# The last three shared tiles of a decoder layer: accumulating transfers in place of read back, addition and store

## The chip, the core and the metric

One core of one Trainium2 chip runs the whole kernel. The metric is the device time of one execution in microseconds. The core's engines work beside each other, each on its own list of instructions: TensorE (PE in the profile; its weight loads are PEld), VectorE (DVE), ScalarE (ACT), GpSimd (POOL) and SyncE (SP), which here does nothing but start transfers. They wait for each other on semaphores. Transfers between the memory outside the core (DRAM here) and the core's own memory (SBUF) are started by SP (the profile's queue q1, "hardware") or by POOL (queue q0, "software": POOL itself first writes the descriptors of the transfer, and the profile shows that time as a busy POOL). Both feed the same 16 DMA engines.

## The reference, cut to what matters

```
x = x + attention(layernorm(x))                 # 16 heads, causal, soft cap, gates
x = x + token_experts(layernorm(x))             # 4 experts, chosen by token id
x = x + moe(layernorm(x))                       # the last stage

def moe(h):                                     # h: 2048 rows of 512
    probs = softmax(h @ gate_w.T)               # 8 experts, the best 2 of each row
    out = silu(h @ shared_gate.T) * (h @ shared_up.T) @ shared_down.T
    y = silu(h @ expert_gate) * (h @ expert_up) @ expert_down
    return out + sum of the 2 chosen y, weighted
```

The output is 2048 x 512 floats. Each of its rows is a sum of four things: the residual x that enters the last stage, the shared expert's row, and two rows of routed experts.

## The kernel before, in words

The 2048 rows are 16 tiles of 128. In the last stage TensorE first computes the up-products of the shared expert for all 16 tiles, then their down-products for 13 of them. `resid` holds x, tile by tile; `shared_add` (DVE) adds the shared row to it out of a PSUM bank, and SP stores the tile to `out`. Then come the routed experts: the chosen rows are sorted by expert into ETILES = 39 tiles of 128. For each of them POOL gathers the rows (`gather`), TensorE computes, ScalarE copies the product to `x3_early`, and POOL adds it to the rows of `out` where it belongs, in DRAM, with an indirect transfer that accumulates (`add_rows`, L866). Each of these adds waits until the one before has landed (`e_added`), since two tiles may hold the same row of the output.

The down-products of three shared tiles are left for the very end (LATE = 3; they are steps n = 13, 14 and 15 of `down_s`, and by `PLACES` they are the tiles 12, 13 and 14 of the output). They fill TensorE while the last routed tiles go through the other engines. Since the routed rows for these three tiles are added in DRAM as well, x for them is stored to `out` early, with one transfer (L687). At the end SP waits for the last of the 39 adds, reads the three tiles back from `out` to `resid` (L701), DVE adds the shared product from its bank (L1555, banks 3, 0 and 1), and SP stores the three tiles again (L704). SP then waits until the three stores have landed, and the program ends.

What sets the order around the change is the order in which each engine's instructions are written, and the semaphores: `e_added` (39 adds, 16 each), `s_y` (a shared down-product is complete in its bank), `s_y_out` (DVE has taken it), `stored` (SP's early stores), `late_loaded` and `late_stored`. No scheduler moves anything.

Of the kernel before, what the change touches and what calls it, by code (L numbers as in the profile page):

```python
# [7 lines left out]
ALU = mybir.AluOpType  # L8
# [6 lines left out]
TILES = T // P  # L15
# [26 lines left out]
EARLY_FROM, LATE_FROM = 6, 12  # L42
LATE = 3
# [4 lines left out]
ETILES = TOPK * T // P + EXPERTS - 1  # L48
# [20 lines left out]
def build(nc, x, token_ids, wqk_in, wv_in, wgates, wo_in, pre, out):  # L69
    with ExitStack() as ctx:  # L70
# [21 lines left out]
        def sem(name):  # L92
            return ctx.enter_context(nc.semaphore(name))

        bank = [ctx.enter_context(nc.psum_tensor(f"bank{i}", [P, 512], F32)) for i in range(8)]
# [3 lines left out]
        resid = sb("resid", [P, TILES, D])  # L99
# [183 lines left out]
        S = {n: sem(n) for n in names.split()}  # L283
# [111 lines left out]
        ov = out[0:T].rearrange("(t p) d -> p t d", p=P)  # L395
# [35 lines left out]
        PLACES = [*range(LATE_FROM), TILES - 1, *range(LATE_FROM, TILES - 1)]  # L431
        LATE_AT = TILES - LATE
        LATE_BANKS = (3, 0, 1)

        def odd(n):

            return FULL_STEPS <= n < LATE_AT and (n - FULL_STEPS) % 2
# [16 lines left out]
        def y_bank(n):  # L454
            if n >= LATE_AT:
                return LATE_BANKS[n - LATE_AT]
            return XT if n >= FULL_STEPS and not odd(n) else YB
# [15 lines left out]
        def _(sp):  # L473
# [181 lines left out]
            def load_expert(e):  # L655
                at = EXP_AT + e * (UP + DOWN)
                if e == 2:
                    sp.wait_ge(S["route_e_done"], 1)
                if e >= 2:
                    tiles_before = sp.value_load(expert_end[0:1, e - 2:e - 1], min_val=1, max_val=ETILES)  # L660
                for part, used, lo, n in (("up", "e_up", 0, UP), ("down", "e_aT_ready", UP, DOWN)):
                    if e:
                        sp.wait_ge(S[f"{part}_loaded"], 16 * e)
                    if e >= 2:
                        sp.wait_ge(S[used], tiles_before + (used == "e_aT_ready"))
                    sp.dma_start(plain(expert_w[:, e % 2, 2 * lo:2 * lo + 2 * n].rearrange("p (l n) -> p l n", l=2)),
                                 pre_parts[:, :, at + lo:at + lo + n]).then_inc(S[f"{part}_loaded"], 16)
# [28 lines left out]
                sp.dma_start(ov[:, PLACES[n], :], resid[:, PLACES[n], :]).then_inc(S["stored"], 16)  # L696
            for e in range(2, EXPERTS):
                load_expert(e)
            sp.wait_ge(S["e_added"], 16 * ETILES)
            for n in range(LATE):  # L700
                sp.dma_start(resid[:, LATE_FROM + n, :], ov[:, LATE_FROM + n, :]).then_inc(S["late_loaded"], 16)  # L701
            for n in range(LATE_AT, TILES):
                sp.wait_ge(S["s_y_out"], n + 1)
                sp.dma_start(ov[:, PLACES[n], :], resid[:, PLACES[n], :]).then_inc(S["late_stored"], 16)  # L704
            sp.wait_ge(S["late_stored"], 16 * LATE)

        @block.gpsimd
        def _(pool):
# [139 lines left out]
            def gather(g):  # L848

                if g < 2:  # L850
                    pool.wait_ge(S["s_xT_ready"], TILES - 1 + g)
                else:
                    pool.wait_ge(S[f"e_row{g % 2}"], 16 * (g // 2))
                before = g - ROW_BUFFERS
                if before >= 0:
                    pool.wait_ge(S["e_xT_ready"], before + 1)
                    if not by_tensor(before):
                        pool.wait_ge(S["e_moved"], before - TB + 1)
                nc.gpsimd.indirect_dma_start(rows_e(g), None, x3_rows, bass.IndirectOffsetOnAxis(ids_e[:, g:g + 1], 0)).then_inc(S[f"e_row{g % 2}"], 16)

            def add_rows(g):

                pool.wait_ge(S["e_y_out"], g + 1)
                if g:
                    pool.wait_ge(S["e_added"], 16 * g)
                nc.gpsimd.indirect_dma_start(out, bass.IndirectOffsetOnAxis(ids_e[:, g:g + 1], 0), x3_early[:, g % E_ROWS, :], None, compute_op=ALU.add).then_inc(S["e_added"], 16)  # L866
# [8 lines left out]
            for g in range(ETILES):  # L875
                if g + ROW_BUFFERS < ETILES:
                    gather(g + ROW_BUFFERS)
                add_rows(g)

        @block.scalar  # L880
        def _(act):
# [289 lines left out]
        def _(dve):  # L1171
# [376 lines left out]
                turn(x3(t)).then_inc(S["s_xT_ready"], 1)  # L1548

            def shared_add(n):  # L1550
                if n >= LATE_AT:
                    dve.wait_ge(S["late_loaded"], 16 * LATE)
                dve.wait_ge(S["s_y"], n + 1)
                row = resid[:, PLACES[n], :]
                nc.vector.tensor_tensor(row, bank[y_bank(n)][:, :], row, ALU.add).then_inc(S["s_y_out"], 1)  # L1555

            def turn_rows_e(t):
# [8 lines left out]
            def step(ph, g, j=0, first=False, last=False, between=None):  # L1566
                W, H = WIDTH[ph], HALVES[ph]
                for i in range(H):
                    dve.wait_ge(S[f"{ph}_silu"], H * g + i + 1)
                    part = act_sb[:, i * W:i * W + W]  # L1570
                    if ph == "e":
                        nc.vector.scalar_tensor_tensor(out=part, in0=bank[1][:, 0:W], scalar=weights_e[:, g:g + 1], in1=part, op0=ALU.mult, op1=ALU.mult).then_inc(S["e_act"], 1)
                    else:
                        nc.vector.tensor_tensor(part, part, bank[X_FIRST if first else 0][:, 0:W], ALU.mult).then_inc(S["x_act"], 1)
                if not last:
                    xT_low(ph, g + 1)
                if ph == "e" and first:
                    shared_add(LATE_AT - 1)
                if between:
                    between()  # L1580
                if ph == "e":
                    weights_ready("down_loaded", g)
                last_x = last and ph == "x"
                parts = LAST_PARTS_X if last_x else aT_parts(ph)
                for n, (c0, c1) in enumerate(parts):
                    w = chunk(ph, c0)[1]
                    of = last_bank(c0, c1) if last_x else aT_bank(ph, c0, c1, w)

                    read = n + 1 if last_x else sum(p[0] // KC <= c0 // KC for p in parts)
                    dve.wait_ge(S[f"{ph}_aT_hi"], len(aT_parts(ph)) * g + read)  # L1590
                    nc.vector.tensor_tensor(aT_lo[0:w, c0:c1, :], of, aT_hi[0:w, c0:c1, :].bitcast(F32), ALU.subtract).then_inc(S[f"{ph}_aT_lo"], 1)
# [80 lines left out]
            def step_s(g):  # L1672
                mult_s(g, 0)
                if g + 1 < TILES:
                    xT_low_s(g + 1)
                mult_s(g, 1)
                if 1 <= g <= FULL_STEPS:
                    shared_add(g - 1)
                if g < FULL_STEPS:
                    aT_low_s(g)  # L1680
                if TURNED_FROM <= g + 2 < TILES:
                    turn_x3(g + 2)
# [105 lines left out]
            choose(FIRST_ROUTED, TILES)  # L1788
            nc.vector.tensor_tensor(by_router.chosen[:, :], choice[0][:, :], choice[1][:, :], ALU.add).then_inc(S["chosen_ready"], 1)
            shared_add(FULL_STEPS)  # L1790
            aT_low_s(FULL_STEPS + 2)
            link(nc.vector.tensor_copy(share_hi[:, :, :], share[:, :, :]))
# [43 lines left out]
        def _(pe):  # L1836
# [220 lines left out]
            def down(ph, g, hi, lo, second, between=None, to=YB, parts=None):  # L2057
                if second:
                    pe.wait_ge(S[f"{ph}_y_out"], g)
                parts = parts or aT_parts(ph)  # L2060
                for c in range(NCH[ph]):
                    w = chunk(ph, c)[1]
                    if c == NCH[ph] - 1 and between:
                        between()
                    for n, (c0, _) in enumerate(parts):
                        if c == c0:
                            pe.wait_ge(S[f"{ph}_aT_lo"], len(aT_parts(ph)) * g + n + 1)
                    last = triple(bank[to][:, :], aT_hi[0:w, c, :], aT_lo[0:w, c, :], hi(c, w), lo(c, w), c == 0, c == NCH[ph] - 1)
                last.then_inc(S[f"{ph}_y"], 1)
# [235 lines left out]
```

## Time and profile before

| | us |
|---|---|
| time before, median of 3 runs | 1555.71 (1552.31 to 1561.29) |
| the profiled execution, its own time | 1548.69 |
| its span | 1546.9 |
| PE busy | 1523.6 (98%) |
| DVE busy | 1163.8 (75%) |
| ACT busy | 655.6 (42%) |
| POOL busy | 454.0 (29%) |
| last matmul started | 1534.94 |
| first instruction of the final exchange (SP, L701) | 1537.84 |

The span is the time from the first to the last instruction in the trace; the execution's own time is 1.8 us longer. Time stamps in this document count from the start of the span. A busy share is an average over the whole span, and says nothing of the last few microseconds, where the change is; those are read from the timeline and the chain of waits.

### The profile page before, as it was taken

Reading aid. Unit: us, or ns where it says so; the run is one execution under the profiler, and the core shown is the slowest. Engines: PE = TensorE matmul, PEld = TensorE weight load, DVE = VectorE, ACT = ScalarE, POOL = GpSimd, SP = SyncE. Lnnn points to the kernel's source line nnn. Section 1 sums busy time; section 2 is a strip of 40 time slices with the busy share of each in tenths; the row PEclk is TensorE's granted clock in tenths of the full one; section 3 lists DMA queues with packets and bytes.
Section 4 is the critical chain, followed back from the end, with each engine's and each line's share of the span. In section 5 each row is a group of like instructions: output and inputs, shape, how many; then the busy total and the mean of one; then the engine's idle time right before and its main releaser. Section 6 shows DMA issues by size and latency. Waiting matters only on the chain.

```text
span 1546.9 us, 24256 instructions
## 1 busy us (share of the span) xinstructions
PE 1523.6 (98%) x7597; PEld 1309.7 (85%) x7598; DVE 1163.8 (75%) x2609; ACT 655.6 (42%) x1277; POOL 454.0 (29%) x391
## 2 busy tenths in 40 slices
PE   8999999999999999999999999999999999999996
PEld 7778888888888888888888888888888889999995
DVE  4898887788887888887888778755663675777772
ACT  4454443444444334444344444333111315666662
POOL 4445332234222233222233231113210003333332
PEclk9999999999999999999999999999999999999998
DMA  8786763687986686885686878376441157778744
GB/s 315 283 307 222 236 230 130 239 310 261 303 302 220 252 315 248 310 315 203 257 308 258 318 278 321 99 227 194 131 153 43 50 211 225 231 232 262 196 80 79
DMA packets 106843, 353.98 MB, mean 229 GB/s; under 512 B 11312, under 2 KB 31792, under 8 KB 101232
## 3 DMA queue, kind: packets, MB, share of 16 engines
q1 hardware_dynamic: 93520, 314.62, 56.0%
q0 software_dynamic: 13216, 38.02, 10.4%
q8 instruction: 57, 0.93, 0.3%
q14 instruction: 50, 0.41, 0.1%
HBM read 228.34 MB, written 124.26 MB: 228 GB/s over the span
## 4 chain that ended last, share of the span: by engine, by line
PE 87%; DMA 5%; DVE 5%; issue 1%; POOL 1%; ACT 1%; SPq 0%; DVEq 0%; POOLq 0%; ACTq 0%
PE bank L399 28%; PE bank L400 28%; PE bank L401 28%; DMA out<-x_early,ids_e 4%; PE bank L2079 1%; DMA wqk<-wqk_parts 1%; PE bank L1910 0%; DMA rows<-x_rows,ids_e 0%; DMA wv_raw<-wv_in 0%; POOL store L721 0%; DVE resid L1555 0%; DVE place_hot L1727 0%; DVE tile_vals L1737 0%; DVE stats L1181 0%; DMA resid<-out 0%
## 5 line engine op out<-in xcount | busy, mean ns | idle before, releaser
L765 POOL TENSOR_TENSOR probs<-probs,causal 128x256 f32<-128x256 f32 x126 | 90.3, 738 | 401.9 <-ACT probs L951 390.6
L399 PE MATMUL bank<-store,wqk 128*128 128x512 f32 x512 | 200.3, 391 | 0.8 <-DMA wqk<-wqk_parts 0.8
L400 PE MATMUL bank<-store,wqk 128*128 128x512 f32 x512 | 200.0, 391 | 0.0
L401 PE MATMUL bank<-store,wqk 128*128 128x512 f32 x512 | 199.2, 389 | 0.0
L1351 DVE SCALAR_TENSOR_TENSOR resid<-bank,factor,resid 128x512 f32<-128x512 f32 x256 | 189.1, 741 | 1.8 <-PE bank L401 1.7
L721 POOL TENSOR_TENSOR pre_split<-pre_raw,pre_split 128x1536 fp32r<-128x1536 f32 x34 | 119.4, 3512 | 137.6 <-ACT pre_split L910 137.6
L949 ACT ACTIVATE probs<-bank 128x512 f32<-128x512 f32 x189 | 86.8, 527 | 128.6 <-PE bank L401 125.7
L401 PEld LDWEIGHTS bank<-store,wqk 128*128 128x128 f32 x512 | 96.2, 188 | 20.5
L399 PEld LDWEIGHTS bank<-store,wqk 128*128 128x128 f32 x512 | 96.3, 188 | 19.7 <-DMA wqk<-wqk_parts 1.2
L1000 ACT ACTIVATE k_hi<-bank 128x512 fp32r<-128x512 f32 x64 | 38.4, 600 | 175.3 <-PE bank L401 175.3
L400 PEld LDWEIGHTS bank<-store,wqk 128*128 128x128 f32 x512 | 96.4, 188 | 17.7
L1379 DVE TRANSPOSE_TENSOR_REDUCE bank<-probs 128x16 f32<-128x512 f32 (+3 forms) x256 | 108.5, 492 | 0.0
L399 PE MATMUL bank<-wo,o_hi 128*128 128x512 f32 x256 | 103.9, 406 | 2.5 <-issue 0.9
L399 PE MATMUL bank<-expert_w,xT_hi 128*128 x312 | 103.8, 333 | 1.1 <-DVE xT_lo L1538 0.8
L866 POOL DMA_INDIRECT out<-x_early,ids_e x39 | 61.6, 1579 | 146.1 <-DMA out<-x_early,ids_e 78.6
L399 PE MATMUL bank<-store 128*128 128x512 f32 x256 | 100.2, 392 | 1.1 <-DVE store L1335 1.1
L400 PE MATMUL bank<-expert_w,xT_hi 128*128 x312 | 100.4, 322 | 0.0
L401 PE MATMUL bank<-expert_w,xT_lo 128*128 x312 | 100.3, 322 | 0.0
L400 PE MATMUL bank<-wo,o_hi 128*128 128x512 f32 x256 | 100.0, 391 | 0.0
L401 PE MATMUL bank<-wo,o_lo 128*128 128x512 f32 x256 | 99.9, 390 | 0.0
L401 PE MATMUL bank<-store 128*128 128x512 f32 x256 | 99.7, 389 | 0.0
L400 PE MATMUL bank<-store 128*128 128x512 f32 x256 | 99.7, 389 | 0.0
(366 smaller groups left out, 3983.3 us busy)
## 6 DMA issues: line engine op xcount, KB each, us to landing
pre_parts<-pre_split SPq DMA_DIRECT2D x34, 1536.0 KB, 6.5
wqk<-wqk_parts SPq DMA_DIRECT2D x96, 512.0 KB, 4.3
pre_raw<-pre SPq DMA_DIRECT2D x34, 768.0 KB, 8.2
store<-wv_parts SPq DMA_DIRECT2D x12, 2048.0 KB, 9.2
wo<-wo_parts SPq DMA_DIRECT2D x48, 512.0 KB, 7.1
expert_w<-pre_parts SPq DMA_DIRECT2D x8, 2816.0 KB, 11.1
wqk_parts<-wqk SPq DMA_DIRECT2D x16, 1024.0 KB, 5.6
expert_w<-pre_parts SPq DMA_DIRECT2D x8, 1536.0 KB
```

What stands on the lines that cost most here:

```text
L399: nc.tensor.matmul(out_ap, a_hi, b_hi, start=first, stop=False)
L400: nc.tensor.matmul(out_ap, a_hi, b_lo, start=False, stop=False)
L401: return nc.tensor.matmul(out_ap, a_lo, b_hi, start=False, stop=last)
L721: nc.gpsimd.tensor_tensor(lo, raw, hi.bitcast(F32), ALU.subtract).then_inc(S[done], 1)
L765: nc.gpsimd.tensor_tensor(diagonal, diagonal, causal[:, :, :], ALU.mult).then_inc(S["masked"], 1)
L866: nc.gpsimd.indirect_dma_start(out, bass.IndirectOffsetOnAxis(ids_e[:, g:g + 1], 0), x3_early[:, g % E_ROWS, :], None, compute_op=ALU.add) ...
L949: nc.scalar.activation(probs[:, lo:lo + n], bank[2 + i][:, 0:n], ACT.Tanh, scale=SCALE / SOFTCAP).then_inc(S["tanh_done"], 1)
L1000: nc.scalar.activation(k_hi[:, :], bank[1][:, :], ACT.Copy).then_inc(S["qk_hi_done"], 1)
L1351: nc.vector.scalar_tensor_tensor(out=row, in0=bank[of][:, :], scalar=factor[:, u % 2, i:i + 1], in1=row, op0=ALU.mult, op1=ALU.add).then_i ...
L1379: last = nc.vector.tensor_reduce(sums[:, j * P // BLOCK:, 0, j], cols, mybir.AxisListType.X, ALU.add, apply_transpose=True)
L2079: last = nc.tensor.transpose(bank[AT + c // KC][0:w, c % KC * P:c % KC * P + P], act_of_chunk(ph, c), ident[:, :])
```

## The change

The read back, the addition on DVE and the plain store of the three late tiles go. Instead DVE copies the shared product from its bank to the tile of `resid` as soon as it is complete (and once the early store of that tile has landed), and POOL, after the last of the 39 adds has landed, starts three direct transfers that accumulate these tiles onto `out` in DRAM. SP only waits for the three transfers.

```diff
@@ -696,12 +696,6 @@
             for e in range(2, EXPERTS):
                 load_expert(e)
-            sp.wait_ge(S["e_added"], 16 * ETILES)
-            for n in range(LATE):
-                sp.dma_start(resid[:, LATE_FROM + n, :], ov[:, LATE_FROM + n, :]).then_inc(S["late_loaded"], 16)
-            for n in range(LATE_AT, TILES):
-                sp.wait_ge(S["s_y_out"], n + 1)
-                sp.dma_start(ov[:, PLACES[n], :], resid[:, PLACES[n], :]).then_inc(S["late_stored"], 16)
             sp.wait_ge(S["late_stored"], 16 * LATE)
@@ -876,6 +870,10 @@
                 add_rows(g)
+            pool.wait_ge(S["e_added"], 16 * ETILES)
+            for n in range(LATE_AT, TILES):
+                pool.wait_ge(S["s_y_out"], n + 1)
+                nc.gpsimd.dma_start(ov[:, PLACES[n], :], resid[:, PLACES[n], :], accum_op=ALU.add).then_inc(S["late_stored"], 16)
@@ -1548,10 +1546,12 @@
             def shared_add(n):
-                if n >= LATE_AT:
-                    dve.wait_ge(S["late_loaded"], 16 * LATE)
                 dve.wait_ge(S["s_y"], n + 1)
                 row = resid[:, PLACES[n], :]
+                if n >= LATE_AT:
+                    dve.wait_ge(S["stored"], 16 * (LATE_AT + 1))
+                    nc.vector.tensor_copy(row, bank[y_bank(n)][:, :]).then_inc(S["s_y_out"], 1)
+                    return
                 nc.vector.tensor_tensor(row, bank[y_bank(n)][:, :], row, ALU.add).then_inc(S["s_y_out"], 1)
```

On SP, at the end of its list, the change takes out the transfers of the final exchange (the difference between before and after):

```order
 L665 REGISTER_ALU [waits down_loaded]
 L666 DMA expert_w<-pre_parts 128x2x1536 [waits e_aT_ready]
-L701 DMA resid<-out 128x512 [waits e_added]
-L701 DMA resid<-out 128x512 x2
-L704 DMA out<-resid 128x512 [waits s_y_out] x3
 L70 UNCONDITIONAL_BRANCH [waits late_stored]
```

Six transfers have gone, three loads and three stores; the last row, which is SP's wait for the end, stays.

On POOL, at the end of its list, before the change (L866 is `add_rows`, L859 `gather`):

```order
L866 DMA out<-x_early,ids_e 2176x512 [waits e_added,e_y_out]
L859 DMA rows<-x_rows,ids_e 128x512 [waits e_moved,e_xT_ready,e_row1]
L866 DMA out<-x_early,ids_e 2176x512 [waits e_added,e_y_out]
L859 DMA rows<-x_rows,ids_e 128x512 [waits e_moved,e_xT_ready,e_row0]
L866 DMA out<-x_early,ids_e 2176x512 [waits e_added,e_y_out] x8
L70 UNCONDITIONAL_BRANCH
```

The same place on POOL after the change, where L860 is `add_rows` and L853 `gather`:

```order
L860 DMA out<-x_early,ids_e 2176x512 [waits e_added,e_y_out]
L853 DMA rows<-x_rows,ids_e 128x512 [waits e_moved,e_xT_ready,e_row0]
L860 DMA out<-x_early,ids_e 2176x512 [waits e_added,e_y_out] x8
L876 DMA out<-resid 128x512 [waits s_y_out,e_added]
L876 DMA out<-resid 128x512 [waits s_y_out] x2
L70 UNCONDITIONAL_BRANCH
```

The three accumulating transfers stand behind everything else that POOL does. On DVE the three additions at the end of its list have become three copies in the same place, and TensorE's and ScalarE's lists are unchanged.

## Rows read from the trace of the kernel before

**Rows 1.** The page: the span, and the busy time of each engine

```profile
span 1546.9 us, 24256 instructions
PE 1523.6 (98%) x7597; PEld 1309.7 (85%) x7598; DVE 1163.8 (75%) x2609; ACT 655.6 (42%) x1277; POOL 454.0 (29%) x391
```

**Rows 2.** Chain that ended last, 1490 to 1548 us: start, length, what

```profile
by line: DMA out<-x_early,ids_e 73.8%; issue 12.1%; DMA resid<-out 6.3%; DVEq L70 1.8%; SPq L701 1.3%; DVE resid L1555 1.1%; POOLq L70 0.4%; POOLq L865 0.2%; DVEq L1553 0.0%
...
1527.80 4.57 DMA out<-x_early,ids_e
...
1533.18 4.64 DMA out<-x_early,ids_e
...
1538.72 3.67 DMA resid<-out
```

**Rows 3.** Timeline of SP, same stretch: start, length, queue, line, what

```profile
1537.84 1.31 SPq L701 DMA_DIRECT2D resid<-out  x3
1543.13 1.53 SPq L704 DMA_DIRECT2D out<-resid  x3
```

**Rows 4.** Line L704, the last stores: durations ns, first and last start; landing

```profile
L704 SPq DMA_DIRECT2D out<-resid x3: 332/338/343, 1543.1 to 1544.3; - x3
...
DMA to landing us min/median/max: 2.0/2.1/2.2
```

**Rows 5.** Timeline of DVE, 1527 to 1548 us

```profile
1529.63 0.89 DVE L1669 TENSOR_TENSOR aT_lo_odd<-bank,aT_hi_odd 128x512 fp32r<-128x512 f32 x2 [4.70 <-ACT aT_hi_odd L1142]
1530.55 0.29 DVE L1670 TENSOR_TENSOR aT_hi_odd<-bank,aT_hi_odd 64x128 fp32r<-64x128 f32 x1
1542.41 1.89 DVE L1555 TENSOR_TENSOR resid<-bank,resid 128x512 f32<-128x512 f32 x3 [11.56 <-DMA resid<-out]
```

**Rows 6.** Timeline of TensorE from 1531 us: tile 14's last matmul, tile 15's last

```profile
1531.09 0.39 PE L2175 MATMUL bank<-sh_down_lo,aT_hi_late 128*128 128x512 f32 x1
...
1534.94 0.39 PE L2175 MATMUL bank<-sh_down_lo,aT_hi_odd 128*128 128x512 f32 x1
```

**Rows 7.** Timeline of POOL, 1505 to 1548 us, the last two adds

```profile
1527.80 1.55 POOL L866 DMA_INDIRECT out<-x_early,ids_e  x1 [4.12 <-DMA out<-x_early,ids_e]
1533.18 1.55 POOL L866 DMA_INDIRECT out<-x_early,ids_e  x1 [3.83 <-DMA out<-x_early,ids_e]
```

**Rows 8.** Line L866, the 39 accumulating adds: POOL ns min/median/max; landing

```profile
L866 POOL DMA_INDIRECT out<-x_early,ids_e x39: 1549/1580/1647, 1287.5 to 1533.2; - x39
...
DMA to landing us min/median/max: 4.5/4.8/10.9
```

**Rows 9.** Line L770, indirect plain stores on POOL, same columns

```profile
L770 POOL DMA_INDIRECT xs<-xrows,slot_x x16: 960/972/1201, 339.5 to 998.1; - x16
```

**Rows 10.** Line L819, direct plain loads of 384 KB on POOL, same columns

```profile
L819 POOL DMA_DIRECT2D sh_down_lo<-pre_parts x4: 546/546/548, 1059.5 to 1066.0; - x4
...
DMA to landing us min/median/max: 3.4/3.9/5.8
```

**Rows 11.** Timeline of POOL, 1040 to 1130 us, a pair of these loads

```profile
1059.48 1.08 POOL L819 DMA_DIRECT2D sh_down_lo<-pre_parts  x2 [4.87 <-DVE bank L1197]
```

**Rows 12.** Timeline of DVE, 1058 to 1060 us, what that pair waited for

```profile
1058.10 1.09 DVE L1197 STREAM_TRANSPOSE bank<-rows 128x512 f32<-128x512 f32 x1
```

**Rows 13.** Engines by stretch; the last two columns: DMA share, GB/s

```profile
1535.30:1537.40 2.10, 0.03 (x1) 0.00 (x0) 0.00 (x0) 0.00 (x0) 0.00 (x0) 1.00 1.02 125
1537.84:1538.84 1.00, 0.00 (x0) 0.00 (x0) 0.00 (x0) 0.00 (x0) 0.00 (x0) 0.58 0.02 6
1538.84:1542.34 3.50, 0.00 (x0) 0.00 (x0) 0.00 (x0) 0.00 (x0) 0.00 (x0) 0.50 0.72 223
1543.80:1546.30 2.50, 0.00 (x0) 0.00 (x0) 0.50 (x1) 0.00 (x0) 0.00 (x0) 0.50 0.85 315
```

**Rows 14.** The last add's transfer in slices of half a microsecond, same columns

```profile
1535.80:1536.30 0.50, 0.00 (x0) 0.00 (x0) 0.00 (x0) 0.00 (x0) 0.00 (x0) 1.00 0.27 49
1536.30:1536.80 0.50, 0.00 (x0) 0.00 (x0) 0.00 (x0) 0.00 (x0) 0.00 (x0) 1.00 1.05 193
1536.80:1537.30 0.50, 0.00 (x0) 0.00 (x0) 0.00 (x0) 0.00 (x0) 0.00 (x0) 1.00 1.01 184
```

## The prediction

> **What bounds the kernel now.** I read the page's span and busy times first, then the chain that ended last, then the timelines of SP, DVE, TensorE and POOL over the last 20 us, and last the lines whose operations resemble the new one. TensorE is busy 98% of 1546.9 us [rows 1], so nearly all of the kernel is its matmuls, and the change leaves its list alone. Its last matmul starts at 1534.94 and lasts 0.39 [rows 6]: some 11.6 us of span lie behind it, in which TensorE does nothing, and the edit is in there.
>
> In the last 57 us the chain runs through the accumulating adds, 73.8% of it [rows 2], one behind another: an add is issued at 1527.80, the next at 1533.18, the engine idle 3.83 us between for the landing [rows 7]. The last lands at 1533.18 + 4.64 = 1537.82 [rows 2]; call it T, since SP starts its first read back at 1537.84 [rows 3]. The sum is made from there, and everything ahead of T is the same in both kernels: the same 39 adds behind the same waits.
>
> The exchange at the end: SP issues three loads from 1537.84 for 1.31 us [rows 3]; the last lands at 1538.72 + 3.67 = 1542.39 [rows 2]; DVE, idle 11.56 us for it, adds three tiles from 1542.41 for 1.89 us [rows 5]; the three stores are issued from 1543.13, the last at 1544.3, and land 2.0 to 2.2 us later [rows 3, 4], so at about 1546.4; the span ends at 1546.9 [rows 1]. So the tail is 1546.9 - 1537.84 = 9.06 us: 4.6 load, 1.9 DVE and the issue of the last store, 2.1 landing, 0.5 from there to the end.
>
> **What goes.** All of the 9.06 us but the last 0.5: 8.6 us. SP's removed wait has nothing behind it but the wait for the end. No load is left to start after T.
>
> **What moves under cover.** The three DVE copies. A copy of 128x512 from a bank is close to the addition of that size, 1.89/3 = 0.63 us [rows 5]. They stand where the additions stood, behind DVE's last split, which ends at 1530.55 + 0.29 = 1530.84 [rows 5]. The first two can run as soon as tile 14's last matmul is over, 1531.09 + 0.39 = 1531.5 [rows 6], the third after 1534.94 + 0.39 = 1535.33, so all are done by about 1536.0 to 1536.1. That is 1.7 us before T, and I put them at nothing; if that cover went, the price would be what the third exceeds T by. The added wait on `stored` asks for the count that the 39 adds wait for as well (L874), and the first of them was issued at 1287.5 [rows 8]: it costs nothing. Three semaphore waits on POOL stand behind all its other work; nobody is queued behind them but the three transfers.
>
> **What is added on the path.** Three direct accumulating transfers of 256 KB. No row of this trace is one; there are indirect accumulating ones (L866), indirect plain ones (L770) and direct plain ones (L819), all on POOL. Four terms:
>
> - From T to POOL's first instruction. Before an add it is 1533.18 minus the landing at 1527.80 + 4.57 = 1532.37: 0.8 us [rows 2]. [...] Bounds 0.3 and 0.8; I take 0.8, the same semaphore on the same engine.
> - Writing descriptors. Direct plain: 0.55 us each, two in 1.08 with no gap [rows 10, 11]. Indirect plain 0.97, indirect accumulating 1.58, the last one 1.55 [rows 7 to 9]: accumulation adds 0.6. So 0.55 + 0.6 = 1.15 us; bounds 0.55 and 1.55.
> - From the end of that to landing. The last add: 4.64 - 1.55 = 3.1 us [rows 2, 7]; the shortest direct load, larger but plain: 3.4 - 0.55 = 2.85 [rows 10]. I take 3.1.
> - What the second and third add. Their descriptors are written while the first is moving, so the spacing is the larger of 1.15 us and what the DMA engines need for one. The last add keeps them active for 2.1 us [rows 13], but not evenly: after a first burst there is a lull of half a microsecond at a share of 0.27, and then they move 184 to 193 GB/s [rows 14]. The lull looks like the first answer to the read of the destination, which a transfer queued behind another need not wait for by itself. At 188 GB/s 262,144 bytes take 1.4 us. Plain stores take 0.85 x 2.5 / 3 = 0.7 us each [rows 13]. Bounds: 0.7 below (a plain transfer's share; with the low descriptor time), 2.1 above if they pipeline; 4.65 if they don't (a rival below). I take 1.4, twice 2.8.
>
> Sum from T: 0.8 + 1.15 + 3.1 + 2.8 = 7.85, with the 0.5 at the end 8.35 us. Against 9.06: -0.7 us. The saving of two dependent round trips (load, then store) is given back by slower descriptors and slower, read-and-write transfers. With all low bounds: 0.3 + 0.55 + 2.85 + 1.4 + 0.5 = 5.6, so -3.5. With the high ones, pipelined: 0.8 + 1.55 + 3.1 + 4.2 + 0.5 = 10.15, so +1.1.
>
> A rule that gives another figure: the Trainium skill, "DMA: Bandwidth & Descriptors", section "Anatomy of one DMA", fits a software-queue transfer as about 2.0 us plus its bytes at 436 GB/s, which would be 2.6 us for 256 KB. This trace disagrees for accumulating ones: none of 39 landed in under 4.5 us [rows 8]. By the rule's figure, with two more at 0.6 us of movement each, an estimate of the tail is 0.8 + 2.6 + 1.2 + 0.5 = 5.1 us, near that of the first rival below.
>
> **Forecast.** The profiled execution's own time is 1548.69; less 0.7 it is 1548.0. It lies 7.0 us under the median of the three runs, so at the level of that median the forecast is 1555.0. The difference is 0.05%: no change that can be told. A measurement of this kernel can tell about 0.5%, 7.8 us, from no change; the three runs before lie 9.0 us apart.
>
> **Rivals.**
>
> 1. *Three accumulates cost hardly more than three plain transfers.* Then the low bounds hold: -3.5 us, 1552.2. For it: the direct form's 0.55 us of descriptors, and the 315 GB/s of the stores' stretch [rows 13]. Against it: each add carries the destination's read too, and ran at 0.6 of that speed [rows 14]. Still under 0.5%.
> 2. *The accumulates serialise.* The engines don't start reading the destination of one before the write of the one before it is confirmed, so each takes its whole 4.65 us: 0.8 + 1.15 + 3.1 + 2 x 4.65 + 0.5 = 14.85, +5.8 us, 1561.5: slower than before. Place: the DMA queue behind POOL's second and third transfer. It decides from a spacing of (9.06 - 0.5 - 5.05) / 2 = 1.75 us up: above that the change loses. For it: no two adds are ever in flight together here, so the trace can't exclude it. Against it: plain software transfers overlap (two loads are issued within 1.08 us and land after 3.9 in the median [rows 10, 11]).
>
>    The Trainium skill, same page, section "Two DMAs through the same engine are not ordered", says that descriptors of one queue start in order but are pipelined, read and write sides apart. By that rule the spacing would stay at 1.4 and not 4.65; no row here shows it for accumulating ones.
> 3. *A direct accumulate is cut into smaller pieces than the indirect one.* Say four times the descriptors, 4.6 us for each: 0.8 + 3 x 4.6 + 3.1 + 0.5 = 18.2, +9.1 us, 1564.8. For it only that no such transfer is in the trace, and that some adds landed after 10.9 us [rows 8]; against it, both sides are whole rows of 2 KB.
> 4. *The change doesn't do what it says*: POOL is late because the third copy is, and T is not what it waits for. The copy has 1.7 us of cover; if TensorE's end moved by that much, both kernels would move alike. Price under 1 us.
>
> **How the numbers follow.** Forecast (tail 7.6 to 10.2 us) 50%, own range 1550 to 1560 with the runs' spread; rival 1, 23%; rival 2, 19%; rival 3, 5%; rival 4, 3%. All mechanisms but the third stay within 7.8 us, so what leads out of "same" is chiefly the spread of runs: of the forecast, about a twelfth to either side; of rival 1 a sixth to the faster side; of rival 2 a quarter to the slower side; of rival 3 two thirds. That gives faster 0.09, slower 0.13, same 0.78. Range: from 1552.2 less some 3 us of spread, to rival 2's 1561.5: 1549 to 1561.5.
>
> **What would show it.** In the profile after: the last add landing with the same distance to TensorE's end; three DVE copies of about 0.63 us done before it; three POOL instructions of 1.1 to 1.2 us, back to back, 0.8 us (or 0.3) behind it; the DMA engines active in one unbroken stretch of some 4 to 5 us (rival 1: 2 to 3; rival 2: three stretches with gaps); the third landing 7.9 us after T; no SP transfer behind the expert weights. The forecast is wrong if the tail is outside 7.6 to 10.2 us, or if the loop of adds itself takes another time.

## The result, and the profile after

| | before | after |
|---|---|---|
| median of 22 runs each, us | 1553.45 (1547.87 to 1561.29) | 1557.80 (1552.24 to 1561.77) |
| ratio, 95% interval | | 1.0027 [1.0016, 1.0038] |
| profiled execution: own time, span, us | 1548.69, 1546.9 | 1557.56, 1555.8 |
| T, landing of the last of the 39 adds | 1537.83 | 1543.18 |
| tail, from T to the end of the span | 9.1 | 12.6 |

The change makes the kernel slower by 0.27%, 4.2 us (2.5 to 5.9), where 0.7 us less was forecast. That is less than the 0.5% that the forecast took for the smallest difference to be told; with 22 runs of each it is clear of noise, and the sign was wrong. The two profiles lie 8.9 us apart, and 3.5 of it is tail. The other 5.4 us is T, and nothing here puts it down to the edit. small_soft, tile_waits, its repeat tile_waits_b, two_queues and small_soft3 below have the kernel before's lists up to T, and their T is 1542.4, 1542.4, 1544.8, 1540.9 and 1548.3, against 1537.8 in the profile of before; load_behind has the changed kernel's lists up to T, and its T is 1537.1. Most of the shift is there before the last adds: TensorE's last matmul starts at 1534.94 before [rows 6] and at 1539.31 after, 4.4 us later.

```profile
1539.31 0.39 PE L2175 MATMUL bank<-sh_down_lo,aT_hi_odd 128*128 128x512 f32 x1
```

What moves TensorE's end and T from one execution to the next was not studied. So everything below is measured from T.

The end of the chain of waits in the changed kernel (start, length, what):

```profile
1538.61 4.57 DMA out<-x_early,ids_e
1543.18 1.17 issue
1544.34 1.88 POOL out L876 x2
1546.22 0.89 POOLq L70
```

It answers to the chain of [rows 2], where the load stood behind the last add. The chain is followed to POOL's third transfer and its closing instruction, 1546.22 + 0.89 = 1547.11, and then stops, 8.7 us ahead of the end: a hint that what comes next isn't an ordinary instruction. POOL's timeline and DVE's, which answer to [rows 7] and [rows 5]:

```profile
1538.61 1.56 POOL L860 DMA_INDIRECT out<-x_early,ids_e  x1 [3.98 <-DMA out<-x_early,ids_e]
1544.34 2.77 POOL L876 DMA_DIRECT2D out<-resid  x3 [4.18 <-issue]
```

```profile
1535.24 1.33 DVE L1553 COPY resid<-bank 128x512 f32<-128x512 f32 x2
1539.73 0.69 DVE L1553 COPY resid<-bank 128x512 f32<-128x512 f32 x1 [3.16 <-PE bank L2175]
```

The copies are done at 1540.42, 2.8 us ahead of T: they cost nothing, as forecast. Line L876 (POOL's time for one in ns, then the time from start to landing), which answers to [rows 8]:

```profile
L876 POOL DMA_DIRECT2D out<-resid x3: 961/1267/1597, 1544.3 to 1545.5; - x3
...
DMA to landing us min/median/max: 3.9/5.3/6.1
```

The three rows of POOL overlap (they start at 1544.34, 1544.96 and 1545.52), so that the three together take 2.77 us and not the sum of their durations. The third is started at 1545.5 and lands 6.1 later, at 1551.6. After that there is nothing to move, and still 4.2 us to the end. The engines and the DMA share by stretch, as in [rows 13] (the DMA engines are active for 5.9 us without a gap, where the forecast said 4 to 5):

```profile
1545.30:1551.20 5.90, 0.00 (x0) 0.00 (x0) 0.00 (x0) 0.00 (x0) 1.81 (x3) 0.50 0.92 133
1551.60:1555.60 4.00, 0.00 (x0) 0.00 (x0) 0.00 (x0) 0.00 (x0) 0.00 (x0) 0.50 0.00 0
```

SP's waits at the end (engine, line, what it waited for: us in total, times, longest) show who is late:

```profile
SPq L70 <- DMA out<-resid: 105.6, 1, 105.6
SPq L70 <- PEq L70: 4.0, 1, 4.0
```

Once the transfers have landed, SP waits another 4.0 us in the barrier that closes the program (L70), where each engine reports after its own drain. In the kernel before, the same row says 0.2. The engine that the row names is a guess by its semaphore; TensorE's last matmul had ended at 1539.7. The rows of line L70 itself (queue, operation, ns, start) say which it was. After, and then before:

```profile
L70 POOLq EVENT_SEMAPHORE  x2: 17/17/17, 1555.6 to 1555.7; - x2
L70 ACTq DRAIN  x1: 901/901/901, 1533.4 to 1533.4; - x1
L70 PEldq DRAIN  x1: 4267/4267/4267, 1535.5 to 1535.5; - x1
L70 DVEq DRAIN  x1: 730/730/730, 1539.7 to 1539.7; - x1
L70 POOLq DRAIN  x1: 10402/10402/10402, 1545.2 to 1545.2; - x1
L70 SPq COMPARE_BRANCH  x1: 37/37/37, 1551.6 to 1551.6; - x1
```

```profile
L70 POOLq EVENT_SEMAPHORE  x2: 17/17/17, 1546.7 to 1546.8; - x2
...
L70 POOLq DRAIN  x1: 8914/8914/8914, 1533.0 to 1533.0; - x1
...
L70 SPq COMPARE_BRANCH  x1: 38/38/38, 1546.5 to 1546.5; - x1
```

POOL's drain stands behind its last transfer in POOL's list in both, though its row begins up to 0.3 us before that transfer's own row. Before, it runs from 1533.0 to 1541.9, four microseconds beyond T, but SP's exchange lasts to 1546.5 and hides it. After, it runs to 1555.6, 4.0 beyond the last landing. The drains of ScalarE, TensorE and DVE had ended by 1540.5, and SP is through its own wait at 1551.6: POOL's is the only one left, and the program ends 0.2 behind it. In all eight profiles of this document in which POOL's drain is the last to end, the span ends 0.23 us behind it. This long row was in the trace of before; it was hidden there, and I didn't ask what hid it.

### The profile page after: what moved, and what is told of

Same layout as the page of the kernel before. It is cut to its first block, busy times and chain, and to the rows that moved or that the text cites. A ratio compares the mean times of both kernels' runs of the same rounds, so it can differ in the third digit from the quotient of the medians.

```text
span 1555.8 us, 24254 instructions
## 1 busy us (share of the span) xinstructions
PE 1525.6 (98%) x7597; PEld 1309.8 (84%) x7598; DVE 1164.5 (75%) x2609; ACT 655.9 (42%) x1277; POOL 457.7 (29%) x394
## 4 chain that ended last, share of the span: by engine, by line
PE 84%; DMA 7%; DVE 5%; issue 2%; POOL 1%; ACT 1%; POOLq 0%; SPq 0%; DVEq 0%; ACTq 0%
PE bank L399 27%; PE bank L400 27%; PE bank L401 27%; DMA out<-x_early,ids_e 5%; DMA wqk<-wqk_parts 1%; PE bank L2079 1%; PE bank L1910 0%; DMA rows<-x_rows,ids_e 0%; DMA wv_raw<-wv_in 0%; POOL store L715 0%; DVE place_hot L1727 0%; DVE tile_vals L1737 0%; DMA x_early<-xs_out,slot_x 0%; DVE resid L1555 0%; PE bank L1853 0%
## 5 line engine op out<-in xcount | busy, mean ns | idle before, releaser
L860 POOL DMA_INDIRECT out<-x_early,ids_e x39 | 61.7, 1583 | 150.5 <-DMA out<-x_early,ids_e 60.5
```

## The experiments

Theory D: the drain is what the tail ends on. Its rival L: the accumulates are just slower than forecast, and the 4 us at the end are not the drain's. F: the drain runs a fixed time from the last descriptors. "Landing" is read from the semaphores; each row of the table is one profiled execution, in us; the tail is from T to the end of the span. The ratios further down are to executions of the kernel before that were timed beside the version in question.

| kernel | last descriptors | last landing | drain ends | behind descriptors | behind landing | tail |
|---|---|---|---|---|---|---|
| before | T - 3.09 | T | T + 4.05 | 7.1 | 4.0 | 9.1 |
| after | T + 3.93 | T + 8.39 | T + 12.41 | 8.5 | 4.0 | 12.6 |
| load_behind | T + 3.94 | T + 9.03 | T + 13.05 | 9.1 | 4.0 | 13.3 |
| small_soft | T + 7.62 | T + 9.01 | T + 14.80 | 7.2 | 5.8 | 15.0 |
| small_soft3 | T + 8.54 | T + 9.85 | T + 15.88 | 7.3 | 6.0 | 16.1 |
| soft_plain | T + 2.77 | T + 4.85 | T + 8.87 | 6.1 | 4.0 | 9.1 |
| soft_one | T + 2.55 | T + 9.41 | T + 13.35 | 10.8 | 3.9 | 13.6 |
| plain_one | T + 2.01 | T + 5.16 | T + 9.09 | 7.1 | 3.9 | 9.3 |
| hard_copy | T - 3.19 | T | T + 3.95 | 7.1 | 3.9 | 4.2 |

Landings here are those of the software queue; hard_copy's and before's later ones are of SP's queue, T + 3.4 and T + 8.7, and the drain takes no notice of them: it ends within 0.1 us of T + 4.0 in both.

One profile of each is little, but the timed runs bear the tails out: in every timed version the difference of its tail to before's lies inside the interval of its ratio. For the changed kernel that is 3.5 us, with 2.5 to 5.9 timed; for load_behind 4.2 (1.2 to 5.9), for small_soft 5.9 (3.3 to 8.9), for soft_one 4.5 (0.2 to 5.6), for hard_copy -4.9 (-8.1 to -3.3).

**load_behind**: something more for SP to do, behind the landing.

```diff
             sp.wait_ge(S["late_stored"], 16 * LATE)
+            sp.dma_start(resid[:, LATE_FROM, :], ov[:, LATE_FROM, :]).then_inc(S["late_loaded"], 16)
+            sp.wait_ge(S["late_loaded"], 16)
```

> The changed kernel, and behind the landing of the three accumulates SP still reads one tile of 256 KB back and waits for it. T is the landing of the last of the 39 adds, the tail is what lies from there to the end of the span; 12.6 us in the changed kernel, 9.06 before. Theory D (POOL's closing instruction, a drain, ends 4.0 us after its last transfer has landed, and the span 0.2 after that): the load of 2.5 to 2.8 us is hidden behind the drain, tail 12.6 within 0.5. Rival L (the slower transfers alone set the end, SP's wait for them is what the end hangs on): the load is paid in full, tail 15.4.

Measured: 1.0023 [1.0008, 1.0038] to before, so as the changed kernel. SP's waits, and POOL's drain:

```profile
SPq L70 <- DMA resid<-out: 2.3, 1, 2.3
SPq L70 <- PEq L70: 1.4, 1, 1.4
```

```profile
L70 POOLq DRAIN  x1: 11035/11035/11035, 1539.1 to 1539.1; - x1
```

SP's load took 2.6 us, and SP still waited 1.4 in the barrier: the load went under the drain, which again ended 4.0 us behind the software landing. That is D, and against L. The tail is 13.3 and not 12.6 because the three accumulates themselves took 0.6 longer to land, at T + 9.03.

**small_soft**: a software transfer nobody needs, at the end of the kernel before.

```diff
                 add_rows(g)
+            pool.wait_ge(S["e_added"], 16 * ETILES)
+            pool.wait_ge(S["s_y_out"], TILES)
+            nc.gpsimd.dma_start(out[T:T + 16], resid[0:16, 0, :]).then_inc(gath[0], 16)
```

> The kernel before, and POOL stores 16 spare rows of 2 KB with its own queue after DVE's last addition (T + 6.5); nobody waits for this transfer but POOL's drain. Theory D: start at T + 7.5, descriptors 0.5, landing some 2 us behind them at T + 10, drain 4.0 more: tail 14 to 14.5, about 5 us slower than before. Rival F (the drain takes a fixed 7.2 to 8.5 us from the last descriptor, whenever the data lands): tail 15.3 to 16.7. Rival L: nothing on the path is longer, tail 9.1 within 0.3.

Measured: 1.0039 [1.0021, 1.0057], 6.1 us slower, with all of the exchange in place. 32 KB did it:

```profile
L881 POOL DMA_DIRECT2D out<-resid x1: 592/592/592, 1549.5 to 1549.5; - x1
DMA to landing us min/median/max: 2.0/2.0/2.0
```

```profile
L70 POOLq DRAIN  x1: 7800/7800/7800, 1549.4 to 1549.4; - x1
```

```profile
SPq L70 <- PEq L70: 6.2, 1, 6.2
```

L is out. But D's 4.0 us behind landing failed too: the drain ended 5.8 behind it, and 7.2 behind the descriptors, close to the 7.1 of the kernel before. The tail of 15.0 lies between what D and F said, and F, one fixed time behind the descriptors, cannot be 7.2 here and 9.1 in load_behind. So there seems to be a floor as well, and the rule that fits these is the later of two times: some 7.1 to 7.2 us behind the last descriptors, 4.0 behind the last landing. Where an indirect add comes last, as in the kernel before, it is the floor that counts. What the drain does in that time no run shows.

**soft_plain**: the changed kernel with `accum_op=ALU.add` taken out.

> The changed kernel with three plain stores in place of the accumulating ones (it leaves out the addition of what stands in the output for these tiles). It prices accumulation. The third landing was at T + 8.4. If my term of the prediction for plain transfers holds: gap 1.0, three times 0.55 us of descriptors, 2.9 to landing, so T + 5.5 to 6, and by theory D a tail of 9.8 to 10.2. If the drain's 4 us belongs to accumulating transfers alone, the tail is 6 to 6.5.

Measured: 0.9994 [0.9980, 1.0009], a tail of 9.1: the level of before. Plain transfers land at T + 4.85 where the accumulating ones land at T + 8.39, and the tail is 3.5 us shorter. Not all of that is shown to be accumulation's: POOL starts 0.35 us behind T here and 1.17 in the changed kernel, and then pauses 0.7 between the first and the second. From POOL's start to the last landing it is 4.5 us against 7.2, 2.7 less; from the start of the third transfer, which the pause brings nearly level (T + 2.23 and T + 2.34), 2.6 against 6.1, 3.4 less. So accumulation costs 2.7 to 3.4 us. The drain still takes its 4.0 behind landing, so it isn't accumulation's. It ends 6.1 behind the descriptors, under the floor, which I had not expected either. POOL's timeline and its drain:

```profile
1543.47 0.62 POOL L876 DMA_DIRECT2D out<-resid  x1 [3.66 <-DMA out<-x_early,ids_e]
1544.79 1.10 POOL L876 DMA_DIRECT2D out<-resid  x2 [0.70 <-issue]
```

```profile
L70 POOLq DRAIN  x1: 6776/6776/6776, 1545.2 to 1545.2; - x1
```

**soft_one**: one accumulating transfer of three tiles.

```diff
-            for n in range(LATE_AT, TILES):
-                pool.wait_ge(S["s_y_out"], n + 1)
-                nc.gpsimd.dma_start(ov[:, PLACES[n], :], resid[:, PLACES[n], :], accum_op=ALU.add).then_inc(S["late_stored"], 16)
+            pool.wait_ge(S["s_y_out"], TILES)
+            nc.gpsimd.dma_start(ov[:, LATE_FROM:LATE_FROM + LATE, :], resid[:, LATE_FROM:LATE_FROM + LATE, :], accum_op=ALU.add).then_inc(S["late_stored"], 16)
```

> The changed kernel with one accumulating transfer of 768 KB for the three tiles. If the spacing of the three is set by what the DMA engines need (1.4 us or more each), the landing stays at T + 8 to 8.5 and the tail at 12.2 to 12.7 by theory D. If it is POOL's descriptor instructions or their starts that space them, it lands a microsecond or more earlier, tail 11 to 11.5.

Measured: 1.0019 [1.0001, 1.0036], and a tail of 13.6, a microsecond more than with three, which neither case had. POOL's descriptors are done in 1.39 us where three instructions took 2.77, so they are not what makes it late; the transfer itself takes longer. Why one is slower than three was not tested. 768 KB land 9.41 us behind T:

```profile
L875 POOL DMA_DIRECT2D out<-resid x1: 1387/1387/1387, 1551.4 to 1551.4; - x1
DMA to landing us min/median/max: 8.3/8.3/8.3
```

**plain_one**: soft_one without the accumulation, executed once.

> soft_plain with one plain store of 768 KB in place of three (it leaves out the addition of what stands in the output for these tiles). Later of 7.18 us from the descriptors' end and 4.0 from landing: landing at T + 4 to 5, about 3.5 behind the descriptors, so the drain ends at T + 8 to 9. As against soft_one (landing T + 9.4), it prices accumulation of 768 KB: 4.5 to 5 us.

Measured: landing at T + 5.16, drain to T + 9.09. Accumulating 768 KB costs 4.25 us (a little under what I expected). POOL starts 1.17 us behind T, as in soft_one and the changed kernel, so that gap is not accumulation's either. Why soft_plain alone starts at T + 0.35 stays open. The drain ended 3.9 behind landing and 7.1 behind the descriptors, both limits at once.

**small_soft3**: small_soft with three transfers of 16 rows, executed once.

> As small_soft, with three small software transfers of 16 rows back to back in place of one. It tells apart two readings of the drains seen so far, which ended 7.18 us after the last descriptors or 4.0 us after the last landing, whichever is later (before, small_soft, soft_one), but 6.1 us after the descriptors in soft_plain. If the floor of 7.18 us falls away with several transfers in flight, the drain ends 4.0 us after the landing, 5.4 to 6 after the descriptors. If it holds, 7.18 after them, and soft_plain has another reason.

Measured: 7.3 us behind the descriptors, 6.0 behind landing. The floor holds with several transfers in flight; why soft_plain went under it stays open.

**hard_copy**: the early DVE copies alone. POOL's block of the change goes, and SP stores the copies.

```diff
+            sp.wait_ge(S["e_added"], 16 * ETILES)
+            for n in range(LATE_AT, TILES):
+                sp.wait_ge(S["s_y_out"], n + 1)
+                sp.dma_start(ov[:, PLACES[n], :], resid[:, PLACES[n], :]).then_inc(S["late_stored"], 16)
```

> One part of the change alone: DVE's early copies stay, but SP stores the three tiles plainly after T (it leaves out the addition of what stands in the output for these tiles). Theory D: the copies are hidden, the stores land at T + 3.0 to 3.3, but the drain of POOL, whose last transfer is the last add, ends at T + 4.1: tail 4.3. Rival L: tail 3.5 to 3.8. Either way T itself does not move.

Measured: 0.9963 [0.9948, 0.9979], tail 4.2 us. SP's last store has landed at T + 3.4, and SP still waits 0.5 for the barrier:

```profile
SPq L70 <- DMA out<-resid: 2.1, 1, 2.1
SPq L70 <- PEq L70: 0.5, 1, 0.5
```

```profile
L70 POOLq DRAIN  x1: 8916/8916/8916, 1539.1 to 1539.1; - x1
```

The drain behind the last add thus sets a floor of about 4.2 us on the tail of any version that ends its adds like this. The copies cost nothing.

**tile_waits**: the kernel before, a semaphore for each load.

```diff
+        late_load = [(S["late_loaded"], 16), (S["ids_loaded"], 32), (S["wg_loaded"], 32)]
...
-                sp.dma_start(resid[:, LATE_FROM + n, :], ov[:, LATE_FROM + n, :]).then_inc(S["late_loaded"], 16)
+                sp.dma_start(resid[:, LATE_FROM + n, :], ov[:, LATE_FROM + n, :]).then_inc(late_load[n][0], 16)
...
-                    dve.wait_ge(S["late_loaded"], 16 * LATE)
+                    dve.wait_ge(*late_load[n - LATE_AT])
```

> The kernel before with a semaphore of its own for each of the three loads, so that DVE adds a tile as soon as that tile is there. Both theories: the first two additions (1.26 us) and their stores go under the loads; the third starts at its load's landing, T + 4.6, lasts 0.65, its store lands 2.5 later, tail 8.2 to 8.4 where before has 9.06. About 0.05% of the time, too little for the timed rounds. By theory D the drain ends at T + 4.1 and doesn't matter.

> tile_waits once more, for more rounds. Its tail was 7.26 us against 9.06: a gain of 1.8 us, 0.12%, if T does not move. Both sets together should lie at 0.9988, with an interval that may still hold 1.

Measured: tails of 7.3 and 7.5 us, better than the 8.2 to 8.4 expected, since the third load landed at T + 4.0 and 4.4 and not 4.6, and the stores 2.0 to 2.1 us behind their start where 2.5 had been put. SP's and DVE's timelines of the first:

```profile
1542.40 1.30 SPq L702 DMA_DIRECT2D resid<-out  x3
1545.84 1.64 SPq L705 DMA_DIRECT2D out<-resid  x3
```

```profile
1545.12 2.00 DVE L1556 TENSOR_TENSOR resid<-bank,resid 128x512 f32<-128x512 f32 x3 [11.78 <-DMA resid<-out]
```

DVE starts 2.7 us behind T where before it started 4.6 behind it [rows 5]. In time: 1.0000 [0.9986, 1.0014] and 0.9991 [0.9976, 1.0005]. The 1.6 to 1.8 us that the traces show are 0.1%; the timed runs agree with them and also with nothing. The two sets average about 0.9996, where 0.9988 was expected. It's the shortest tail among the versions that compute the right output, and not shown to be faster.

**two_queues**: tile_waits, with the middle tile's load and store in ScalarE's queue.

> As the kernel before with a semaphore for each load, and ScalarE starts the middle tile's load and store in its own queue beside SP's. Loads start 0.4 us sooner (SP's three issues took 1.31 us), the last lands at about T + 4.1 if the DMA engines are not what bounds them: tail 7.7 to 8.2. If they are, it is as with one queue, 8.2 to 8.4.

Measured: 0.9995 [0.9976, 1.0013], tail 8.0. As expected in size, and in this one profile worse than one queue: SP's first load took 3.4 us instead of 2.7 to land, and DVE began 3.5 us behind T; the last load landed at T + 4.4, no sooner than with one queue. I put that down to the loads sharing the DMA engines, which no run tests.

## Why the prediction was wrong

- **T is the same in both kernels**: not contradicted, as far as the spread lets one see. The sign named for it, the same distance from TensorE's end to T, did not come: 2.5 us before and 3.5 after. But that distance runs from 2.5 to 5.6 us over the twelve profiles, so it could not serve as a sign.
- **The copies under cover**: right. 2.8 us of cover, and hard_copy shows them free.
- **From T to POOL's first instruction, 0.8 us**: 1.17, over its upper bound. The rows of the indirect adds did not carry over. No run shows the low bound of 0.3 for an accumulating transfer: all start at T + 1.17, and only the plain ones of soft_plain come near it, with 0.35.
- **Descriptors, 1.15 us each**: the three take 2.77 together, 0.92 each, inside the bounds.
- **End of descriptors to landing, 3.1 us**: the first lands 3.92 behind its start, 2.96 behind its 0.96 of descriptors. Right.
- **Spacing, 1.4 us twice**: 2.0 and 1.3 in the changed kernel, 2.3 and 1.4 in load_behind. So 3.3 to 3.7 for 2.8, and one of the four over the upper bound of 2.1; rival 2, full serialisation at 4.65, is out. The rule cited for it, from the Trainium skill ("DMA: Bandwidth & Descriptors", "Two DMAs through the same engine are not ordered"), agrees with these spacings: accumulating transfers of one queue overlap as well.
- The sum of these, 7.85 to the last landing, came out at 8.39, and 9.03 in load_behind: 0.5 to 1.2 us low.
- **"The 0.5 at the end"**: the step that failed. I took the end of the span to be 0.5 us behind the last landing, because it was so in the kernel before, where the last landing is of SP's queue. The changed kernel's last landing is of POOL's, and POOL's drain ends 4.0 us behind it, and the span 0.2 later: 4.2 us instead of 0.5, 3.7 too few. Forecast 8.35; plus 3.7 for the end and 0.5 for the transfers is 12.6, the tail measured. The error of the transfers alone would have left a tail of 8.9 us (9.5 with load_behind's landings) beside before's 9.1; it is the end that makes the change slower. I had listed what the removed exchange costs and what the new transfers cost, and not what the exchange had been hiding.
- **Rival 2's bound**, that above a spacing of 1.75 us the change loses, used the same 0.5: with a mean spacing of 1.65 it should have won by 0.2 us. (In load_behind the mean is 1.86, beyond the bound.) **Rival 1**'s low transfers nearly occurred in soft_plain (landing at T + 4.85), with a tail of 9.1 instead of 5.6: even plain transfers of the software queue gained nothing here.

On the fit that the prediction cited, 2.0 us plus bytes at 436 GB/s (the Trainium skill, "DMA: Bandwidth & Descriptors", "Anatomy of one DMA"): plain software transfers agree, 2.4 to 2.6 us from start to landing for 256 KB in soft_plain, where it gives 2.6; accumulating ones do not, 3.9 at the least.

## What to carry to other kernels

Before a tail is shortened, read the closing rows of every engine, hidden ones too: the end is the latest of all of them. In this kernel POOL's drain ended 3.9 to 6.0 us behind the landing of POOL's last transfer, and in eleven of twelve profiles no less than 7.1 behind its descriptors; where it was the last to end, the program ended 0.2 after it; behind a last transfer in SP's queue it was 0.4 us, once POOL's drain was over. So an accumulating transfer can save a load and an addition only where something else ends later than its drain. At the very end of this kernel, loads, additions and stores that wait tile by tile left the shorter tail: 7.3 and 7.5 us against 12.6.

## What the runs showed that I had not expected

- POOL's drain lasts 8.9 us in all five profiles where an indirect add is its last transfer (8914 or 8916 ns), and ends 7.14 us behind that add's descriptors in each, wherever SP's last store lands.
- Behind a transfer of 32 KB that nobody waits for, the drain holds the program's end back as well, by 5.9 us of tail.
- One accumulating transfer of 768 KB is slower than three of 256 KB: 8.3 us from start to landing, against 1551.57 - 1544.34 = 7.2 for the three.
- Accumulation costs 2.7 to 3.4 us on three tiles in three transfers, and 4.25 in one.
